# Graph layers over a 0/1 adjacency: columns 1 and 2 leave the Sign check of the first pass, 20 more tiles are checked in the third

## The reference

```python
h = relu(layernorm(x))
x1 = swish((adj @ h) @ W0 + b0)
x = x + swish((adj @ x1) @ W0 + b0)
h = relu(layernorm(x))
a = adj + eye(8192)
d = a.sum(axis=1) ** -0.5
x = x + ((a * d[:, None] * d[None, :]) @ h) @ W1.T + b1
```

## Time and profile before

| | us |
|---|---|
| median of 3 runs | 1447.41 (1445.41 to 1447.41) |
| the profiled execution | 1448.34 |
| its span | 1444.9 |
| TensorE busy | 1384.5 (96%) |
| DVE busy | 1011.8 (70%) |
| ACT busy | 684.1 (47%) |

### The profile page before, as it was taken

The page is one execution under the profiler, slowest core; times in us unless marked ns, Lnnn a source line. Parts: engine busy times, 40 slices in busy tenths (PEclk is TensorE's granted clock), DMA queues, the critical chain, the costliest instruction groups (busy, mean ns, idle before and its releaser), DMA issues.

```text
span 1444.9 us, 18304 instructions
## 1 busy us (share of the span) xinstructions
PE 1384.5 (96%) x6598; PEld 649.3 (45%) x6598; DVE 1011.8 (70%) x2334; ACT 684.1 (47%) x781; POOL 33.9 (2%) x30
## 2 busy tenths in 40 slices
PE   3778999999999999999999999999999999999998
PEld 1333444444444444444444454454444444444444
DVE  7978888899988786786774777877565555546331
ACT  7788878788777667656560112222311221132000
POOL 1100000000000000000000011101000000000000
PEclk9999999999999999999999999999999999999999
DMA  9999999999999898886760111111433233333000
GB/s 378 358 413 408 409 410 403 401 399 399 395 376 387 320 356 318 331 365 263 296 273 29 37 51 66 67 52 62 178 124 146 110 132 137 134 118 123 23 15 24
DMA packets 56255, 335.49 MB, mean 232 GB/s; under 512 B 6240, under 2 KB 6752, under 8 KB 18272
## 3 DMA queue, kind: packets, MB, share of 16 engines
q1 hardware_dynamic: 49104, 322.20, 56.7%
q10 hardware_dynamic: 7056, 12.06, 2.2%
HBM read 322.44 MB, written 11.80 MB: 231 GB/s over the span
## 4 chain that ended last, share of the span: by engine, by line
PE 78%; DMA 10%; DVE 8%; issue 3%; ACT 2%; DVEq 0%; ACTq 0%; SPq 0%
PE acc_ps L586 21%; PE acc_ps L587 21%; DMA ring<-adj 9%; PE acc_ps L527 9%; PE acc_ps L528 9%; PE early_ps L496 6%; PE early_ps L497 6%; PE z_ps L479 3%; DVE marks L843 2%; PE kept_ps L505 2%; PE kept_ps L506 2%; ACT marks L662 1%; DVE stats L822 1%; ACT unused L707 1%; DVE node_a L836 1%
## 5 line engine op out<-in xcount | busy, mean ns | idle before, releaser
L707 ACT ACTIVATE unused<-ring 128x2048 uint8<-128x2048 uint32 x220 | 420.0, 1909 | 92.3 <-DMA ring<-adj 82.4
L527 PE MATMUL acc_ps<-marks,node_a 128*128 128x512 fp8e4 x1024 | 392.0, 383 | 52.7 <-DVE node_a L836 31.2
L528 PE MATMUL acc_ps<-marks,node_a 128*128 128x512 fp8e4 x1024 | 392.1, 383 | 1.8 <-issue 1.8
L586 PE MATMUL acc_ps<-ring,node_a 128*128 128x512 fp8e4 x1024 | 388.1, 379 | 0.0
L587 PE MATMUL acc_ps<-ring,node_a 128*128 128x512 fp8e4 x1024 | 388.1, 379 | 0.0
L843 DVE TENSOR_SCALAR marks<-ring 128x2048 uint8<-128x2048 f32 x226 | 277.0, 1226 | 70.7 <-DMA ring<-adj 41.5
L343 DVE TENSOR_SCALAR ring<-bits 128x256 uint32<-128x256 uint32 (+1 forms) x784 | 159.3, 276 | 89.6 <-PE acc_ps L587 89.5
L527 PEld LDWEIGHTS acc_ps<-marks,node_a 128*128 128x128 f16 x1024 | 100.9, 98 | 188.8 <-issue 74.4
L748 ACT ACTIVATE nT<-acc_ps 128x512 f32<-128x512 f32 x16 | 9.6, 597 | 313.3 <-PE acc_ps L587 313.3
L496 PE MATMUL early_ps<-marks,node_b 128*128 128x512 fp8e4 x416 | 157.7, 379 | 0.0
L497 PE MATMUL early_ps<-marks,node_b 128*128 128x512 fp8e5 x416 | 157.7, 379 | 0.0
(11 more groups left out here) (117 smaller groups left out, 1107.3 us busy)
## 6 DMA issues: line engine op xcount, KB each, us to landing
ring<-adj SPq DMA_DIRECT2D x256, 1024.0 KB, 7.5
marks<-adj SPq DMA_DIRECT2D x36, 1024.0 KB, 5.0
node_b<-x SPq DMA_DIRECT2D x4, 1024.0 KB, 13.0
xch<-x SPq DMA_DIRECT2D x16, 256.0 KB, 2.8
xn_scratch<-xnew ACTq DMA_DIRECT2D x16, 256.0 KB, 2.0
xch<-xn_scratch SPq DMA_DIRECT2D x16, 256.0 KB, 2.9
out<-xnew ACTq DMA_DIRECT2D x16, 256.0 KB, 2.0
part_scratch<-stage ACTq DMA_DIRECT2D x13, 256.0 KB, 5.1
```

What stands on the lines that cost most here:

```text
L527: nc.tensor.matmul(acc_ps[c % 2][:, :], hi_of(node_a16, j), byte, start=(j == 0), stop=False)
L528: last = nc.tensor.matmul(acc_ps[c % 2][:, :], lo_of(node_a16, j), byte, start=False, stop=(j == NB - 1))
L586: nc.tensor.matmul(into[:, :], hi_of(node, j), byte.bitcast(E4), start=opens, stop=False)
L707: nc.scalar.activation(unused[:, :], slot(g).bitcast(U32), ACT.Sign, accum_out=nz_count[:, g:g + 1]).then_inc(counted, 1)
```

## The change

Both lists and the number of late tiles per column are changed, and `compare_counts` takes its slices of the counts accordingly:

```diff
-ACT_MARKED = [0, 1, 2, 3, 4, 5, 7, 9, 11, 13] + [TC + i for i in range(1, TC, 2)] + [g for g in range(2 * TC, 5 * TC) if g % 4 == 3]
-LATE = list(range(TC)) + ACT_MARKED[10:]
-LATE_STEP = 3
+ACT_MARKED = [0, 1, 2, 3, 4, 5, 7, 9, 11, 13] + [g for g in range(TC, 3 * TC) if g % 2 == 1] + [g for g in range(3 * TC, 5 * TC) if g % 4 == 3]
+LATE = list(range(3 * TC)) + [g for g in ACT_MARKED if g >= 3 * TC]
+LATE_STEP = 4
...
-                for of in (nz_count[:, 0:TC], nz_count[:, TC:2 * TC].rearrange("p (i s) -> p i s", s=2)[:, :, 1],
-                           nz_count[:, 2 * TC:5 * TC].rearrange("p (i s) -> p i s", s=4)[:, :, 3]):
+                for of in (nz_count[:, 0:3 * TC],
+                           nz_count[:, 3 * TC:5 * TC].rearrange("p (i s) -> p i s", s=4)[:, :, 3]):
```

## The result

The changed kernel takes 1464.95 us (median of 4 runs, 1463.18 to 1466.43) against 1446.41 us before (1445.37 to 1447.41): 18.5 us slower, ratio 1.0128, 95% interval 1.0114 to 1.0142. That is inside the forecast range (1458.8 to 1468.0), 1.6 us above the forecast value. The profiled execution took 1463.18 us with a span of 1461.3; its pair before took 1448.34 with 1444.9, so the two profiles stand 16.4 us of span apart.

The account below looks back on a forecast made before the run. Bounds: adj loading in first-pass columns 1 and 2, TensorE in the third pass. Terms -0.5 + 0 + 0 + 14.3 + 2.1 = +15.9 us took the profiled 1448.34 to 1464.2, hence a median of 1463.3 us, range 1458.8 to 1468.0.

Parts of the forecast that it names:

- The wait at L566: Third pass, between columns 13 and 14: TensorE waits for the last group's check and compare, 14.3 us (13.8 to 15.5).
- the landing of the fourth load: Third pass, after column 13's end (T0): the last group's fourth load lands at T0+9.7, right behind the third.
- The clock: Third pass, behind TensorE's wait: matmuls run at half clock for a while, costing 2.1 us (0 to 3.3).
- The first pass: Columns 1 and 2 without Signs: 0.5 us gained, between 2.7 gained and 0.5 lost.
- the transfer sets the pace: First pass, columns 1 and 2: loading of adj is the bound, DMA share 1.00, a tile every 2.48 us.
- rival 1: First pass: slots, not the transfer, set the pace; 9.1 us gained, 1454.7 us in all; chance 0.05 beside the wait.
- Four checks per column: Third pass: a fourth check in each column costs 0 us, at most 1.5, with 1.4 us of cover in the first.
- the second (DVE doesn't hold four checks): Third pass: TensorE waits for an unpacked piece in each of 13 columns; 1470 us at 0.5 us beyond cover; chance 0.05.
- The third (2.7 us of cadence): First pass, columns 1 and 2: the lost cadence comes back whole, 2.7 us instead of 0.5; 1461.1 us; chance 0.12.

Follow-up runs that it names:

- third_only: Kernel before the change with only the third pass changed (56 tiles checked, four per column; first pass as before): 1462.82 us against 1445.85, ratio 1.0116.
- warm: Changed kernel with 62 needless TensorE matmuls ahead of its wait at L566: 1461.46 us, ratio 1.0106 to the kernel before.
- two_in_last: Changed kernel checking 54 of 56 late tiles, so the last group has two instead of four: 1456.76 us, ratio 1.0070 to the kernel before.
- first_only: Changed kernel's first pass, but the third checks only 36 tiles, three per column, leaving out 20 of columns 1 and 2: 1444.10 us against 1445.85 before.
- no_signs_1_to_5: Changed first pass with no Sign in columns 0 to 5; third pass checks 36 tiles, 60 left out: 1443.56 us against 1445.93 before.
- before_longer_act: Kernel before the change with 16 needless waits in ACT's program ahead of the third pass (1392 instructions instead of 1384): 1447.67 us against 1445.64.
- before_60_waits: Kernel before the change with 60 needless waits in ACT's program ahead of the third pass (1414 instructions instead of 1384): 1446.73 us against 1445.89.
- compare_later: Changed kernel with the compare and TensorE's small matmul over it one column later, all 56 tiles checked: 1446.84 us against 1445.85 before, ratio 1.0009.
- five_per_column: Changed kernel with five late tiles per column instead of four, so the 56 are through with column 11: 1450.67 us against 1445.64 before.

## Why the prediction was right

By its own steps:

- **The wait at L566** (14.3 us, from 13.8 to 15.5): TensorE stands for 14.8 us in the changed kernel and 14.7 in third_only. The prediction's term goes to the first matmul of column 14, the small matmul included, and by that measure it is 15.1 us: the 16.7 us of the place less 1.6 of clock. The step that made it so long was read from the code, as the last group of 56 = 14 x 4 and the order of ACT, and the rows of a quieter column gave its length. Off was the landing of the fourth load, T0+10.6 instead of T0+9.7, which was taken from the spacing of two loads that left together. It took 5.9 us from its start, where the earlier trace rows give 4.73 for one alone (the prediction has 4.71); the third took 4.8. That is no accident of this column: in columns 1 to 12 of the same profile the fourth load took 5.2 to 6.7 us. What makes it longer (the third load, the output store) was not taken apart.
- **The clock** (2.1 us, 0 to 3.3): 1.6 in the changed kernel, by its rows and by warm. Counted in the same way it is 2.8 us in third_only (thirteen steps), 2.3 in two_in_last (ten), and the earlier trace rows have 1.7 and 2.6. The length of the gap doesn't order them: 14.8, 14.7 and 6.4 us. All lie within the bounds; how near the 2.1 comes to one of them is luck.
- **The first pass** (0.5 us gained, from 2.7 to -0.5): 0.7 by the spans of first_only, hardly above the noise. That the transfer sets the pace is borne out by no_signs_1_to_5: 60 Signs less, 1.05 us. The one pair of profiles was misleading here: the first pass (the copy of its last sums) ends at 772.95 instead of 776.43, 3.5 us sooner, which is the very sign that the prediction named for rival 1. The same row in the other profiles with the first pass of before is at 774.61, 772.30 and 772.88, and in the six others with that of the change between 771.42 and 775.76; the means are 774.1 and 773.3.
- **Four checks per column** (0, at most 1.5): 0, with 0.26 us to spare in the first column where 1.4 were forecast. The difference is again the fourth load: it landed 3.65 us after the third and not 2.48.
- **What was missing**: ACT's last jump. In the changed kernel's span it costs 2.7 us (3.1 instead of 0.4 from the branch to the next instruction), and outside the span 1.3 us are gained (1.9 instead of 3.2), 1.4 together. The two kernels that differ from before in nothing else lie on both sides of that: 2.0 us more in before_longer_act, 0.8 in before_60_waits. The 0.4 us that are left of the 3.1 are the last stores, 3.2 us from DVE's last instruction to ACT's last wait instead of 2.8; in the other profiles this is 2.7 to 3.1, so it is chance. The sum is then 15.1 + 1.6 - 0.7 + 1.4 = 17.4, against 18.5 measured (16.5 to 20.5 by the interval). The prediction's 15.9 lacked this term and 0.8 of the wait, and had 0.5 too much for the clock. That it came within 1.6 us although a term was missing is in part luck: of the 2.7 us that the jump costs in the span, half came back outside it.

Of the rivals, the first (the slots set the pace) falls with no_signs_1_to_5, the second (DVE doesn't hold four checks) by compare_later, and by five_per_column for a steady column even with five. The third (2.7 us of cadence) is not borne out: 0.7.

**Still open** is which places in ACT's program are bad. Between 1386 and 1392 instructions the end goes from 3.8 to 6.7 us, and between 1414 and 1422 back to 4.0; the time outside the span falls somewhere between 1386 and 1392 too. It is high in the four kernels of 1384 and 1386 instructions alone, and only in their profiles another packet of queue 14 starts 2.5 to 3.4 us after the end of the span; in the ten others the last one starts within 0.6 us of it. That the length of ACT's program does it is shown by before_longer_act and before_60_waits, in which nothing else differs. That ACT waits there for instructions is what the packets of queue 14 say: in the six profiles with a long end its next instruction comes only after the second has landed. It isn't shown by a run that changes the fetch alone. On this the Trainium skill has a rule, in "Runtime: NRT & Kernel Launch", section "Instruction fetch mechanics": instructions are fetched in order, in blocks of 256, and a taken branch whose target isn't in the two blocks at hand has to wait for a DMA. The runs agree in kind (2.7 us lost at some places of the jump and none at others, with two packets of 8 KB behind the branch); they don't show the period.

## What to carry to other kernels

A check or sum that is allowed "somewhere late" still has a last member: before spreading more of it, follow the last one to the first instruction that waits for it, on the engine that sets the time. Here moving two steps by one column (compare_later) took back the 16.8 us of that place. Where an engine's busy time falls by a third or more and the time doesn't (ACT in columns 1 and 2), the other bound (here the DMA share of 1.00) had said so before; and one pair of profiles can differ by 3.5 us where the medians differ by less than 1.

## What was not expected of the hardware

- 8 more instructions on an engine that idles at the end cost 2.0 us (before_longer_act, 1.0013), by their place and not by their work: 2.6 us in the span, behind ACT's last jump, less 1.3 outside it. With 60 such waits (before_60_waits) it was 0.8 us, which can't be told from none.
- Two loads of 1 MB that start 2.1 us apart need longer than one alone (4.7 us): in columns 1 to 13 of the changed kernel the first took 4.8 to 5.1 us, the second 5.2 to 6.7.
- Gaps of TensorE of 2.07, 6.4, 14.7 and 14.8 us were followed by 8, 10, 13 and 7 steps between matmuls at half clock, which cost 1.6 to 2.8 us. 62 needless matmuls in the gap save them (1.6 us in the changed kernel).
